# The last head and its key and query columns in one 272-column projection, keys turned on TensorE, key broadcast by graph

## The reference

```python
# layer 0
h = maximum(layernorm(x), 0)
x = x + (adj @ (h @ W0) + bias0)
# layer 1: 8 heads of 256 columns
h = maximum(layernorm(x), 0)
g = h @ fc_w + fc_b                         # [128, 8, 256]
q, k = g @ q_w + q_b, g @ k_w + k_b         # one number per node and head
logits = leaky_relu(q + k.T + (1 - adj) * -1e9, 0.01)
out = softmax(logits) @ g                   # per head
x = x + sigmoid(concat_heads(out) @ fp_w + fp_b + h)
```

## Time and profile before

| | |
|---|---|
| Time, median of 3 runs | 1406.16 us (1406.15 to 1406.91) |
| Span of the profiled execution | 1404.9 us |
| PE busy | 1394.7 us (99%) |
| DVE busy | 1285.1 us (91%) |
| ACT busy | 1126.5 us (80%) |
| POOL busy | 1102.0 us (78%) |
| Mean share of the DMA queue q1 | 30.3% |

### The profile page before, as it was taken

How to read it: one execution, slowest core, us unless ns; L and a number is a source line. 1 busy time by engine, 2 the same in 40 slices (tenths; PEclk the granted TensorE clock), 3 DMA queues, 4 the chain that set the end, 5 groups by cost and what they waited for, 6 DMA issues and landing times.

```text
span 1404.9 us, 31603 instructions
## 1 busy us (share of the span) xinstructions
PE 1394.7 (99%) x9048; PEld 1252.5 (89%) x9048; DVE 1285.1 (91%) x4408; ACT 1126.5 (80%) x3429; POOL 1102.0 (78%) x1295
## 2 busy tenths in 40 slices
PE   9999999999999999999999999999999999999998
PEld 7898899899899889998998898998989989988987
DVE  7999999999999999999999999999999999998996
ACT  4878788788888888887888888888878878887876
POOL 4788878878778878778787788787787887888764
PEclk9999999999999999999999999999999999999999
DMA  7423323323223233233232232232332322322221
GB/s 238 98 63 107 107 54 106 91 69 106 71 88 106 55 105 106 54 105 97 63 106 80 79 106 61 99 106 54 105 103 58 106 88 73 106 67 85 77 61 41
DMA packets 177132, 124.69 MB, mean 89 GB/s; under 512 B 137808, under 2 KB 143568, under 8 KB 177104
## 3 DMA queue, kind: packets, MB, share of 16 engines
q1 hardware_dynamic: 176816, 124.35, 30.3%
q10 hardware_dynamic: 288, 0.01, 0.0%
HBM read 105.98 MB, written 18.35 MB: 89 GB/s over the span
## 4 chain that ended last, share of the span: by engine, by line
PE 94%; POOL 2%; issue 1%; DVE 1%; DMA 1%; ACT 0%; POOLq 0%; SPq 0%; ACTq 0%; DVEq 0%
PE gbank L381 48%; PE ybank L381 24%; PE tbank L481 8%; PE bank L381 6%; PE bank L426 4%; PE bank L462 2%; PE bank L449 2%; DMA late<-key_rows 0%; POOL att L1561 0%; POOL att L1554 0%; DMA qk<-qk_w_dram 0%; DVE att L829 0%; POOL xb L1544 0%; POOL t_pos L1546 0%; POOL ends L1577 0%
## 5 line engine op out<-in xcount | busy, mean ns | idle before, releaser
L1233 ACT ACTIVATE att<-att 128x128 f32<-128x128 f32 x1024 | 397.8, 393 | 47.0 <-DVE att L836 44.0
L381 PE MATMUL gbank<-m_hi,hT_lo 128*128 128x512 f32 x1024 | 426.7, 417 | 0.0
L1554 POOL TENSOR_TENSOR att<-late,t_pos 128x512 f32<-128x512 f32 x256 | 330.6, 1293 | 120.5 <-PE tbank L481 115.8
L381 PE MATMUL gbank<-m_hi,hT_hi 128*128 128x512 f32 x1024 | 403.2, 394 | 0.0
L381 PE MATMUL gbank<-m_lo,hT_hi 128*128 128x512 f32 x1024 | 401.3, 392 | 0.0
L812 DVE TENSOR_TENSOR g_lo<-gbank,g_hi 128x512 fp32r<-128x512 f32 x512 | 341.4, 678 | 47.1 <-ACT g_hi L1226 42.0
L1561 POOL TENSOR_TENSOR att<-att,rinv 128x512 f32<-128x512 f32 x256 | 289.4, 1131 | 107.1 <-DVE rinv L841 106.5
L1226 ACT ACTIVATE g_hi<-gbank 128x512 fp32r<-128x512 f32 x512 | 291.1, 595 | 39.6 <-PE gbank L381 39.4
L829 DVE TENSOR_SCALAR_CACHE_REDUCE att<-att,qs 128x128 f32<-128x128 f32 x1024 | 291.6, 341 | 27.0 <-POOL att L1554 26.7
L381 PE MATMUL ybank<-g_hi,pT_hi 128*128 128x256 f32 x1016 | 281.5, 277 | 0.0
L381 PE MATMUL ybank<-g_hi,pT_lo 128*128 128x256 f32 x1016 | 281.4, 277 | 0.0
(11 more groups left out here) (97 smaller groups left out, 2323.1 us busy)
## 6 DMA issues: line engine op xcount, KB each, us to landing
late<-key_rows SPq DMA_DIRECT2D x64, 1024.0 KB, 6.1
g_in<-graph_dram SPq DMA_DIRECT2D x64, 512.0 KB, 3.4
out_dram<-ends SPq DMA_DIRECT2D x63, 256.0 KB, 3.9
qs<-key_rows SPq DMA_DIRECT2D x128, 4.0 KB, 2.5
key_rows<-kq_sb SPq DMA_DIRECT2D x64, 24.0 KB, 1.4
att<-fc_wT_dram SPq DMA_DIRECT2D x4, 256.0 KB, 5.6
late<-fp_w_dram SPq DMA_DIRECT2D x4, 256.0 KB, 5.3
ends<-fp_w_dram SPq DMA_DIRECT2D x2, 512.0 KB, 7.9
```

The costliest lines, as they stand in the source:

```text
L381: mm = pe.matmul(out_ap, w, m, start=first and n == 0, stop=last and n == len(terms) - 1)
L1233: e = act.activation(a[:, s], a[:, s], ACT.Exp, scale=-1.0, bias=a[:, CH + h:CH + h + 1], accum_out=esum[j][c][:, h:h + 1])
L1554: gp.tensor_tensor(a, keys[q][:, j, c * HC:(c + 1) * HC, :], t_pos[q][:, j, :].unsqueeze(1).broadcast_to([P, HC, P]), ALU.add)\
```

## The change

The seven first heads stay in `m`; the last head and the 16 key and query columns stand beside each other in `n`, 272 columns. `last_head` computes them for one graph, in `bank1` for graph 0 (`HERE`) and in a bank of the ring for graph 1 (`THERE`), one pair ahead of the rest. The pieces of a graph are then three of 512 columns less one head: A0, A1, A2 and B0, B1, B2 are heads 0 to 5, and `SIXTH` is head 6 of both graphs in one bank. The bias is a row, queries stay in columns where the product leaves them, the keys are turned into 16 rows by one transpose (`turn_keys`) and copied out by DVE (`key_rows_out`). The broadcast is one DMA of 512 KB for each graph.

```diff
-RING = ((7, -1), (1, 0), (2, 0), (3, 0), (0, 0), (4, 0), (6, 0), (5, 0))
+A0, A1, A2, B0, B1, B2, SIXTH = range(7)
+HERE, THERE = 7, 8
+LAST = (HERE, THERE)
+RING = ((B0, -1), (A1, 0), (A2, 0), (THERE, 1), (A0, 0), (SIXTH, 0), (B2, 0), (B1, 0))
+BEFORE = ((A0, A1), (A2, SIXTH, HERE)), ((B0, B1), (B2, SIXTH, THERE))
...
 # SP
-                sp.wait_ge(v_kq, p + 1)
-                sp.dma_start(key_rows[q][0:HALF + ROWS], kq_sb[q][0:HALF + ROWS]).then_inc(s_rows, 16)
+                sp.wait_ge(v_rows, p + 1)
+                sp.dma_start(key_rows[q], rows[:]).then_inc(s_rows, 16)
...
-            def queries_in(p, q):
-                for j in range(J):
-                    sp.dma_start(qs[q][:, j, :], rows, allow_slow_non_contiguous=True).then_inc(s_queries[j], 16)
...
             def step(i, q):
                 load(i + 3, q)
-                keys_in(i - 1, (q + 2) % U)
+                keys_in(i - 1, (q + 2) % U, 0)
+                keys_in(i - 1, (q + 2) % U, 1)
                 store(i - 3)
                 keys_out(i, q)
-                queries_in(i, q)
...
 # TensorE
+            def turn_keys(p, q):
+                for j in range(J):
+                    pe.wait_ge(v_kq[j], p + 1)
+                pe.wait_ge(v_g[HERE], p + 1)
+                pe.transpose(turned, kq_sb[q][:, 0, :, :].rearrange("p j h -> p (j h)"), ident[:]).then_inc(pe_turn, 1)
...
-                for dt in range(DT):
-                    for h in (hT_lo, hT_hi):
-                        mm = pe.matmul(kq.rearrange("r (j n) -> r j n", j=J), u[:, dt, :], h[q][:, dt, :, :], ...)
+            def last_head(p, q, j):
+                bank = here if j == 0 else ring_free(THERE, p)
+                split(bank[:, 0:WIDE],
+                      [((hT_hi[q][:, dt, j, :], hT_lo[q][:, dt, j, :]), (n_hi[:, dt, 0:WIDE], n_lo[:, dt, 0:WIDE]))
+                       for dt in range(DT)]).then_inc(pe_g[LAST[j]], 1)
...
+            def sixth_heads(p, q):
+                bank = ring_free(SIXTH, p)
+                s = slice(6 * D, 7 * D)
+                for j in range(J):
+                    mm = split(bank[:, j * D:(j + 1) * D],
+                               [((hT_hi[q][:, dt, j, :], hT_lo[q][:, dt, j, :]), (m_hi[:, dt, s], m_lo[:, dt, s]))
+                                for dt in range(DT)])
...
             def step(i, q):
-                project(i, q, 2)
+                project(i, q, A2)
                 h_ready(i + 1)
-                queries_keys(i + 1, (q + 1) % U)
-                project(i, q, 3)
-                attend(i - 1, 1, 0)
-                project(i, q, 0)
-                attend(i - 1, 1, 1)
-                transpose_p(i, 0, 0)
-                project(i, q, 4)
-                project(i, q, 6)
+                last_head(i + 1, (q + 1) % U, 0)
+                last_head(i + 1, (q + 1) % U, 1)
+                attend(i - 1, (q + 2) % U, 1, 0)
+                turn_keys(i + 1, (q + 1) % U)
+                project(i, q, A0)
+                attend(i - 1, (q + 2) % U, 1, 1)
+                transpose_p(i, 0, 0)
+                sixth_heads(i, q)
+                project(i, q, B2)
...
 # VectorE
-            def keys_queries(p, q):
-                dve.wait_ge(a_kq, p + 1)
+            def keys_queries(p, q, j):
+                dve.wait_ge(a_g[LAST[j]], p + 1)
+                dve.tensor_tensor(kq_sb[q][:, :, j, :], last_bank(j, p)[:, D:WIDE].rearrange("p (k h) -> p k h", k=2),
+                                  kq_bias[:].rearrange("p (k h) -> p k h", k=2), ALU.add).then_inc(v_kq[j], 1)
+
+            def key_rows_out(p):
+                dve.wait_ge(pe_turn, p + 1)
+                dve.tensor_copy(rows[:], turned).then_inc(v_rows, 1)
+
+            def last_low(p, q, j):
+                dve.wait_ge(a_g[LAST[j]], p + 1)
+                dve.tensor_tensor(last_lo[q][:, j, :], last_bank(j, p)[:, 0:D], last_hi[q][:, j, :].bitcast(F32),
+                                  ALU.subtract).then_inc(v_g[LAST[j]], 1)
...
             def step(i, q):
                 mask_min(i, q, 1, 1)
-                keys_queries(i + 1, (q + 1) % U)
+                keys_queries(i + 1, (q + 1) % U, 0)
+                last_low(i + 1, (q + 1) % U, 0)
                 inverse(i, 0, 0)
                 leaky(i, 0, 1)
+                keys_queries(i + 1, (q + 1) % U, 1)
                 pT_low(i - 1, 1, 1)
-                g_low(i, 1)
+                g_low(i, A1)
+                key_rows_out(i + 1)
...
                 pT_low(i, 0, 0)
-                g_low(i, 3)
-                g_low(i, 0)
+                last_low(i + 1, (q + 1) % U, 1)
+                g_low(i, A0)
...
 # ScalarE
+            def last_high(p, q, j):
+                act.wait_ge(pe_g[LAST[j]], p + 1)
+                act.activation(last_hi[q][:, j, :], last_bank(j, p)[:, 0:D], ACT.Copy).then_inc(a_g[LAST[j]], 1)
...
             def step(i, q):
-                g_high(i, 2)
-                kq_rows(i + 1)
+                g_high(i, A2)
+                last_high(i + 1, (q + 1) % U, 0)
                 pT_high(i - 1, 1, 1)
-                g_high(i, 1)
-                g_high(i, 3)
+                g_high(i, A1)
+                last_high(i + 1, (q + 1) % U, 1)
                 exp(i, 0, 1)
-                g_high(i, 0)
+                g_high(i, A0)
...
 # GpSimd
             def mask_keys(p, q, j, c):
-                gp.wait_ge(s_keys, 16 * (p + 1))
+                gp.wait_ge(s_keys[j], 16 * (p + 1))
```

More of the change, by code:

```diff
@@ L411, in output_bias @@
                 pe.wait_ge(v_cpart, H * DT)
[L412 removed]
+                pe.matmul(ybank[:, 0:D], ones[:], c_part, start=True, stop=True).then_inc(pe_crow, 1)
             def ring_free(n, p):
@@ L955, in begin @@
                 mask_min(1, 1, 1, 0)
-                g_low(1, 2)
+                g_low(1, A2)
+                keys_queries(2, 2, 1)
+                last_low(2, 2, 1)
                 inverse(1, 0, 1)
+                key_rows_out(2)
                 leaky(1, 1, 0)
@@ L1123, in finish @@
                 leaky(62, 1, 0)
-                g_low(62, 2)
-                g_low(62, 3)
-                g_low(62, 0)
+                g_low(62, A2)
+                keys_queries(63, 0, 1)
+                last_low(63, 0, 1)
+                g_low(62, A0)
+                key_rows_out(63)
                 leaky(62, 1, 1)
```

711 lines of the change are left out of this document (359 added, 352 removed).

## The result

The changed kernel takes 1423.1 us (median, 1422.78 to 1423.81), the kernel before 1406.2 in the same session: ratio 1.012, 95% interval 1.0105 to 1.0134. It is 1.2% slower; forecast were 1397.2 us and a range of 1387 to 1408. The span of the profiled execution is 1421.5 us, 16.6 more than before.

A forecast was written before the change was run, and what follows sets the result against it. TensorE, busy 99% of the span, was taken as the bound. Work saved 16.2 us, less 5.7 for the wait at `turn_keys`, 0.5 at the start and 1.0 at the end: 9.0 less, 1397.2 us; range 1387 to 1408.

The forecast's parts named there:

- net 0.24 us for each pair, if nothing waits: TensorE's work in a pair: 1.398 us saved less 1.16 added, net 0.24 us shorter without waits.
- the last heads are 1.50 and not 1.45: TensorE's two `last_head` of a pair: 12 matmuls of 272 columns at 0.121, 1.45 us.
- the turn 0.11 and not 0.18: Lone fp32 transpose `turn_keys`: 0.09 us plus 0.09 for the way back to fp32r, 0.18; bounds 0.11 and 0.27.
- twelve of 256 columns 1.36, that is 0.1137 each: Unit price of TensorE's 256-column matmuls, read as distances in the chain of the kernel before: 0.1137 us each.
- 512 columns cost 2.02 times what 256 do: Claim from the kernel before's rows that TensorE matmuls carry no price on their number.
- TensorE then waits 0.1 us in every pair: Wait at `turn_keys` for graph 1's keys, behind ScalarE's copies: 0.1 us a pair, 5.7 us in the loop's 57 pairs.
- The wait is hidden: Rival: no wait at `turn_keys`, so the saving comes in full, 1386.5 to 1394 us; chance 0.30.
- 1.0 us (0 to 2): Loss in `finish()`: `key_rows_out(62)` blocks VectorE until `turn_keys(62)`, and a bank comes late, once.
- For the start 0.5 was forecast: Start: `key_rows_out(1)` stands ahead of VectorE's first mask, so that chain ends about 0.5 us later.
- 16.2 - 5.7 - 7.6: 16.2 us: TensorE work saved over all pairs; 5.7 us: the wait at `turn_keys` in the loop's 57 pairs.
- The rival on the slow side: Rival *Slower*: ScalarE's copies don't overlap around the new one, wait 0.35 us a pair, 1411.5 us; chance 0.12.

The follow-up runs named there:

- b2: Kernel before with a lone fp32 transpose of 16 identity columns, result unused, ahead of piece 0 in each loop step: 1424.6 us.
- b3: Kernel before with two groups of six 272-column matmuls, results unused, ahead of `queries_keys` in each loop step: 1505.2 us.
- b1: Kernel before with one 512-column piece of each loop pair issued as two trains of six 256-column matmuls: 1409.4 us.
- v4: Changed kernel with `finish()` reordered, `begin()` reordered in pairs 2 and 3, transposes side by side in the loop, and three more moves outside it: 1407.2 us.
- v1: Kernel before with one line moved in TensorE's loop: `transpose_p(i-1,1,1)` right behind `transpose_h(i+1)`, ahead of piece 1: 1412.8 us.
- e2: Changed kernel with piece A0 moved ahead of `attend(i-1,1,0)` and `turn_keys` in the loop: 1427.9 us.
- e5: Changed kernel with `finish()` reordered and `begin()` too, A0 ahead of the next pair's last heads in pairs 0, 2 and 3: 1416.8 us.
- t1: Changed kernel with `finish()` reordered and TensorE's loop cut in ten stretches, eight with small unused additions: 1424.1 us, one execution.

## Why the prediction was wrong

- **The count of the work was right.** "net 0.24 us for each pair, if nothing waits": at 113 ns a pair would be 21.18 us, forecast 21.19. Within it two sizes were off and nearly cancel: the last heads are 1.50 and not 1.45, the turn 0.11 and not 0.18, the lower bound, which I had read from the chain and not taken.
- **The step that failed in the loop is the unit price: "twelve of 256 columns 1.36, that is 0.1137 each".** I took it from a kernel in which all long trains stand at the lower of two distances, and held that it stays, for the new sixth heads and for the untouched attends and transforms, which the sum as a difference leaves at no change. What came is 0.1178 for 5.25 of the six trains of a pair. "512 columns cost 2.02 times what 256 do" is true at that lower distance alone (229 to 113.4); at the other it is 1.94. The row against it was among mine: the four of `queries_keys` at 0.47, 0.1175 each, to be read as "64 weight columns" or as a second distance; I asked neither. The greater distance brought 0.28 us a pair, more than the net gain of 0.24. b2 and b3 show that the lone transpose and the 272 columns each do this alone, b1 that the 256-column train in place of a piece does not.
- The Trainium skill's rule (N/2.4 GHz plus about 2.5 ns for each matmul, TensorE: Matmul & The Clock Gate, "Wait — 56ns, not 53.3ns?") gives, as an estimate, 109 ns for 256 columns and 216 for 512. The traces disagree: they have 113 or 118, and 229. Its direction, which I set aside, holds where trains stand at 118: two of 256 are then 6.6 ns dearer than one of 512 (235.6 for 229). At 113 it doesn't.
- **"TensorE then waits 0.1 us in every pair" did not come.** ScalarE and VectorE were as late as forecast, 2.63 us behind the first last head against 2.59. TensorE was later: the two last heads took 0.05 us more than priced and the attend behind them, at 118 ns, 0.05, and the weight load asked 0.04 ahead of the transpose instead of 0.10. So TensorE did not wait, but came as late, at 2.91, as it would have with the forecast wait: the 0.1 was spent on dearer matmuls. The rival *The wait is hidden*, chance 0.30, named the late weight load as one of its conditions; its time, 1386.5 to 1394, fell with the same price.
- **"1.0 us (0 to 2)" for the end is the other large miss: 9.2.** I looked for the stall at `key_rows_out(62)` on VectorE. It was one engine earlier: `last_high(62,1)` behind two `exp` on ScalarE. I had walked that chain for the loop and not for `finish()`, where its order differs. The new order of `finish()` took back 6.6 us of it in v4, with the lower clock in it. For the start 0.5 was forecast, 5.35 came, and v4 took back 4.8: the last heads of the next pair need `hT_low` earlier than `queries_keys` did, because A0 (once two pieces) no longer stands ahead of them.
- Together: 9.6 us in the 54 pairs of the loop (forecast -7.6, measured +2.0), 8.2 and 4.9 at the ends, and the 2.9 that I had counted as saved outside these pairs (16.2 - 5.7 - 7.6): 25.6, the whole miss in the span (-9.0 forecast, +16.6 measured).
- **The rival on the slow side** had the wrong mechanism (a wait of 0.35 at the turn) and 1411.5. No rival had "an untouched instruction gets dearer" or "the ends are badly ordered", and so the range ended at 1408.
- VectorE, ScalarE, SP and POOL cost nothing in the loop, as forecast.

What stays open: why a train takes one distance or the other. The traces give what precedes it (the distance from the last 512-column matmul ahead), not what makes that distance; nor can I say from them which order would bring all trains of the changed kernel to 113.

## What to carry to other kernels

Where TensorE is the bound without a gap, compare the distance from start to start of *unchanged* groups in both traces before looking for waits: 4.4 ns on each of some 3500 matmuls was more than the net gain planned for the loop. Don't price a new order from a kernel in which the matmuls happen to run at their best distance; take the dearest distance that the trace shows for that size as the other end of the range. And read hand-written prologues and epilogues as carefully as the loop: 14.6 of the 16.6 us were there, and moving lines took back 11.4 of them.

## What the runs showed of the hardware

- Trains of 256-column matmuls have two distances, 113.4 and 117.8 ns, at the same granted clock of 1.00. Once at one, a train keeps it to its end. A train behind a 512-column matmul is at 113 when its first matmul stands 231 to 233 ns behind that one, and at 118 at 225 to 230 (3726 trains in 16 traces).
- A lone fp32 transpose of 16 weight columns costs 0.11 us, but turned three to four later trains to the greater distance, 0.31 us a pair (b2); moving four transposes beside four others did the same to two trains (v1).
- An fp32 group has no cost of its own for the way back to fp32r: the last transpose stands 0.03 ahead of the next matmul, and that one takes 0.32 instead of 0.23, together the 0.109 that a transpose takes among its kind, to within 0.01. Two groups side by side saved 0.03 us a pair (v1, once its trains are counted), not 0.09.
- The same wait can leave TensorE's granted clock alone or be followed by the lower level. After the waits of 3.0 to 3.3 us of the old `finish()` the clock was at 0.50 for 3.4 to 6.8 us in all four traces; after the wait of 2.0 us in the start, in one (e2) of the six kernels that have it; after one of 1.9 us in e5, for 3.4 us.
- A lone fp32r matmul of 64 columns costs about as much as one of 256: 0.11 us (t1).
